# Decoder kernel: gates and scan of the next group moved between the down products, in buffers of their own

## The reference, cut

```
xn = rmsnorm(x);  left = gelu(xn @ left_W)
r = conv4(xn @ right_W)                 # causal, depthwise
a = exp(-8 softplus(a_param) * sigmoid(r @ ga_W));  i = sigmoid(r @ gx_W)
h_t = a_t h_(t-1) + sqrt(1 - a_t^2) * (i_t * r_t)   # scan along the sequence
x1 = left * h @ out_W + x
y  = (gelu(x1n @ up1_W) * (x1n @ up2_W)) @ down_W + x1 ;  x2 = layernorm(y)

kv = products of ctx features in heads of 8;  conv over 128 positions with a
per-head kernel;  out = sum with the query x2 ;  x3 = layernorm(x2 + out)

scores = softmax(x3 @ gate_w.T); top 6 of 64 experts, 64 tokens an expert;
shared expert (352 wide, silu) + 64 experts (176 wide); layernorm
```

## Time and profile before

| | us |
|---|---|
| median of 3 runs | 564.67 (563.73 to 568.37) |
| the profiled execution | 562.52, its span 560.7 |
| TensorE busy | 516.0 (92%) |
| VectorE busy | 377.3 (67%) |
| ScalarE busy | 216.9 (39%) |
| POOL busy | 193.1 (34%) |
| mean granted clock | 0.986 |

### The profile page before, as it was taken

The page is one execution under the profiler, slowest core; times in us unless marked ns, Lnnn a source line. Parts: engine busy times, 40 slices in busy tenths (PEclk is TensorE's granted clock), DMA queues, the critical chain, the costliest instruction groups (busy, mean ns, idle before and its releaser), DMA issues.

```text
span 560.7 us, 6906 instructions
## 1 busy us (share of the span) xinstructions
PE 516.0 (92%) x2211; PEld 317.7 (57%) x2211; DVE 377.3 (67%) x953; ACT 216.9 (39%) x440; POOL 193.1 (34%) x236
## 2 busy tenths in 40 slices
PE   7999999999999799999979999987879999998876
PEld 3438466754766554587744668754444555554565
DVE  2653246759775959786877975899855666663296
ACT  5484135722346841225844114610303333332043
POOL 4703400139024237021507303100026677744250
PEclk9999999999999989999989999998998999999999
DMA  7900993000001100010700010599997999996997
GB/s 269 338 3 23 414 402 136 1 25 13 2 0 39 56 15 23 1 39 0 249 1 1 0 37 2 193 316 294 272 264 231 322 337 331 317 314 221 374 417 260
DMA packets 39894, 91.83 MB, mean 164 GB/s; under 512 B 4513, under 2 KB 24385, under 8 KB 39729
## 3 DMA queue, kind: packets, MB, share of 16 engines
q1 hardware_dynamic: 34864, 75.45, 40.4%
q0 software_dynamic: 4992, 15.93, 8.8%
HBM read 67.02 MB, written 24.34 MB: 163 GB/s over the span
## 4 chain that ended last, share of the span: by engine, by line
PE 65%; DVE 22%; DMA 5%; issue 5%; ACT 2%; SPq 1%; POOL 0%; DVEq 0%; POOLq 0%
PE mb L781 17%; PE mb L1080 8%; PE kb L974 8%; DMA arena<-y_dram 4%; PE kb L1100 4%; PE kb L920 3%; PE kb L1098 3%; PE kb L809 2%; DVE arena L1160 2%; PE mb L787 2%; PE tb L787 2%; DVE arena L1146 2%; PE kb L800 2%; PE mb L800 2%; PE mb L832 2%
## 5 line engine op out<-in xcount | busy, mean ns | idle before, releaser
L781 PE MATMUL mb<-arena 128*128 128x512 f32 x320 | 140.2, 594 | 6.1 <-DVE arena L1201 5.4
L781 PEld LDWEIGHTS mb<-arena 128*128 128x128 f32 x320 | 60.3, 190 | 78.2 <-issue 69.6
L443 POOL TENSOR_TENSOR arena<-arena 128x256 f32<-128x256 f32 (+7 forms) x128 | 80.9, 665 | 66.2 <-PE mb L834 66.2
L673 ACT ACTIVATE arena<-mb,cols 128x512 f32<-128x512 f32 x24 | 16.5, 687 | 78.0 <-PE mb L781 77.9
L974 PE MATMUL kb<-arena 128*128 128x256 f32 x192 | 44.2, 381 | 1.9 <-DVE arena L1389 1.7
L974 PEld LDWEIGHTS kb<-arena 128*128 128x128 f32 x192 | 35.5, 190 | 9.5 <-DVE arena L1389 4.6
L1080 PE MATMUL mb<-arena,x3T 128*64 128x352 f32 x224 | 39.3, 472 | 0.0
L507 POOL DMA_INDIRECT y_dram<-shh,y_all x32 | 32.2, 1008 | 19.9 <-DVE shh L1539 12.2
L468 POOL TENSOR_TENSOR arena<-arena 128x1024 f32<-128x1024 f32 x4 | 9.4, 2350 | 84.6 <-DVE arena L1196 58.9
L1160 DVE TENSOR_TENSOR arena<-arena 128x1024 f32<-128x1024 f32 x28 | 35.9, 1284 | 0.5
L1389 DVE SCALAR_TENSOR_TENSOR arena<-mb,cols,arena 128x512 f32<-128x512 f32 x24 | 17.9, 744 | 24.0 <-PE mb L781 24.0
(11 more groups left out here) (243 smaller groups left out, 1016.3 us busy)
## 6 DMA issues: line engine op xcount, KB each, us to landing
arena<-in_w_experts_dram SPq DMA_DIRECT2D x28, 704.0 KB, 14.8
y_dram<-zeros SPq DMA_DIRECT2D x16, 768.0 KB, 11.0
arena<-y_dram SPq DMA_DIRECT2D x16, 768.0 KB, 16.7
arena<-in_w_experts_down_dram SPq DMA_DIRECT2D x56, 128.0 KB, 13.9
rows_dram<-rows POOLq DMA_DIRECT2D x4, 768.0 KB, 7.0
wextra<-in_w_experts_dram SPq DMA_DIRECT2D x4, 704.0 KB, 6.5
arena<-in_w_experts_down_dram SPq DMA_DIRECT2D x28, 96.0 KB, 14.6
arena<-in_x_dram SPq DMA_DIRECT2D x4, 512.0 KB, 3.6
```

The source lines that it names most:

```text
L443: last = e.tensor_tensor(v.kv[:, hb % 2, :, :, DOFF[d] * NB:DOFF[d] * NB + n], cx[:, :, :, 0:n], cx[:, :, :, d * NB:d * NB + n], ALU.mult)
L781: last = e.matmul(bank, w[:, c, n0:n0 + P], rhs[:, c, :], start=(c == 0), stop=(c == C - 1))
```

## The change

The gates, recurrence and scan of the next group run at the end of a step, in buffers of their own (in `wextra`, where the first two expert weights are loaded later, so these loads now wait for the last scan). A step opens with shared_up 0 (or three fillers), x2's transposes and the out products; heads 8 to 15 follow them. Shared_up 1 and 2 follow x1's transposes. The eight rounds of a group are spread: four in the up stretch of VectorE, four behind `residual(0)`. `products(gt, 3)` runs in the next step's beginning, `biased` before `products(gh, 2)`, and load_ctx follows load_x in SP's queue. PSUM banks are dealt out anew to fit. Group 0's gates and scan stay in step 0.

```diff
-        v.ri = v.mlp[:, 0:4, :]
-        v.th = v.mlp[:, 4:6, :]
+        at[0] = 0
+        v.ri = take(2 * C * TG, wextra).rearrange("p (c n) -> p c n", c=2 * C)
+        v.th = take(C * TG, wextra).rearrange("p (c n) -> p c n", c=C)
+        v.hs = take(C * TG, wextra).rearrange("p (c n) -> p c n", c=C)
@@ sync_program
-                wait(e, s["xs_s"], 2 * g)
+                wait(e, s["xs_s"], 2 * g - 1)
...
-        load_ctx(1)
         for g in range(2, G):
             load_x(g)
-            load_ctx(g)
+            load_ctx(g - 1)
+        load_ctx(G - 1)
...
+        e.wait_ge(s["lr_s"], C * G)
         for p in range(2):
             load_pair(p, v.ring[p], f"load{p}")
@@ pool_program, step
+            if gt is not None:
+                if gh is not None:
+                    wait(e, s["x2_s"], 4 * gh)
+                products(gt, 3)
...
+                if gh + 1 < G:
+                    wait(e, s["xs_s"], 2 * gh + 2)
+                    biased(gh + 1)
...
                 products(gh, 2)
-                products(gh, 3)
-                if gh + 1 < G:
-                    biased(gh + 1)
@@ act_program, step: order of a full step now
   sdA, chances(gs) [Exp of the logits], silu_shared 0, table, mean_square(x1), rms2,
   conv_out(gt, 8..15), norm_root(gh+1), silu_shared 1 and 2, 6 Gelu, conv_out(gh, 0..1),
   sdB, left_right(gh+1), conv_out(gh, 2..3), recurrence(gh+1) [sigmoids, Tanh, Exp],
   x3T copies, roots(gh+1), conv_out(gh, 4..7)
@@ pe_program, step
             if head and tail:
+                wait(e, s["gate_s"], 4 * gh + 4)
+                wait(e, s["conv_evac"], HEADS * gt + 8)
+                if gs is not None:
+                    shared_up(gs, 0, [(s["gate_s"], 4 * gh + 4)] * 2, head)
+                else:
+                    keep_clock(mb[2], 3)
                 x2_transposes()
...
                 wait(e, s["lr_s"], C * gh + C)
                 e.wait_ge(s["w_out"], 16)
-                if tail:
-                    wait(e, s["conv_evac"], HEADS * gt + 14)
+                wait(e, s["y_s"], 2 * gh)
...
+                    for h in range(8, 16):
+                        if h >= 12:
+                            wait(e, s["conv_evac"], HEADS * gt + h - 3)
+                        elif h >= 10 and gs is not None:
+                            wait(e, s["shg_s"] if h == 10 else s["shh_s"], NF * gs + 1)
+                        conv(gt, h)
...
+            if head and gh + 1 < G:
+                features(gh + 1)
             (transposes of the query result, heads 0 and 1)
                 if gh + 1 < G:
+                    if tail:
+                        wait(e, s["conv_evac"], HEADS * gh + 2)
+                    left_right(gh + 1)
                 down([(0, 1)], True)
...
+                    conv(gh, 2)
+                    conv(gh, 3)
+                if gh + 1 < G:
+                    gates(gh + 1)
                 down([(1, 0)], False)
             (x3's transposes, logits, heads 4 to 7, each behind gate_s)
                 down([(1, 1)], True)
@@ dve_program, step
             if head:
+                x1_sum(0)
                 if gs is not None:
+                    shared_rows(gs, 0, head)
+                x1_sum(1)
+                (the query's two copies)
...
+                    if j == 4 and gh + 1 < G:
+                        norm_one(gh + 1)
...
+                    if gs is not None and j < 4:
+                        rounds(j, j + 1)
...
             if head:
                 residual(0)
             if gs is not None:
+                rounds(4, 8)
                 keep_first()
+            if head and gh + 1 < G:
+                recurrence(gh + 1)
             (the logits' maximum)
+            if head and gh + 1 < G:
+                scan(gh + 1, 0)
             if head:
                 n = hsteps.did(residual(1))
             (statistics, lnA_s)
+            if head and gh + 1 < G:
+                scan(gh + 1, 1)
```

More of the change, by code:

```diff
@@ L653, in step @@
                     silu_shared(gs, 1, head)
+                    silu_shared(gs, 2, head)
             if head:
@@ L696, in step @@
                         .then_inc(s["x3T_s"], 1)
+            if head and gh + 1 < G:
+                roots(gh + 1)
             if head and tail:
-                conv_out(gh, 6)
-                conv_out(gh, 7)
-            if tail:
-                wait(e, s["logit_read"], gt + 1)
-                e.activation(v.logit[:], v.logit[:], ACT.Exp).then_inc(s["exp_s"], 1)
+                for h in range(4, 8):
+                    conv_out(gh, h)
+            if tail and not head:
+                chances(gt)
         over_groups(e, step)
@@ L888, in step @@
                 votes_by_expert(gs)
-            if gs is not None and head:
-                shared_up(gs, 0, [(s["q_s"], 2 * gt + 2)] * 2, head)
-                wait(e, s["conv_evac"], HEADS * gt + 15)
-                wait(e, s["dve_r"], RDVE * gt)
-                votes_by_expert(gs, head)
-            elif gs is not None:
+            if gs is not None and not head:
                 for f in range(2):
@@ L940, in step @@
                     transposes(v.xn, k, "x1_tr")
+                if gs is not None:
+                    shared_up(gs, 1, [(s["x1_s"], 2 * gh + 2)] * 2, head)
                 if not tail:
@@ L946, in step @@
                 e.wait_ge(s["w_up"], 16)
+                if gs is not None:
+                    shared_up(gs, 2, [(s["x1T_s"], 4 * gh + 4)] * 2, head)
                 for j in range(FJ):
@@ new lines, in scan @@
+            def scan(g, c):
+                a, i = v.ri[:, 0:2, :], v.ri[:, 2:4, :]
+                wait(e, s["mult_s"], C * g + c + 1)
+                n = csteps.did(e.tensor_tensor(v.th[:, c, :], v.th[:, c, :], i[:, c, :], ALU.mult))
+                wait(e, csteps.sem, n)
+                n = csteps.did(e.tensor_tensor_scan(v.hs[:, c, :], a[:, c, :], v.th[:, c, :], 0.0, ALU.mult, ALU.add))
+                wait(e, csteps.sem, n)
+                wait(e, s["left_s"], 2 * g + c + 1)
+                e.tensor_tensor(v.left[:, c, :], v.left[:, c, :], v.hs[:, c, :], ALU.mult).then_inc(s["lr_s"], 1)
@@ L1315, in step, with x1_sum @@
+            def x1_sum(k):
+                wait(e, s["out_done"], 2 * gh + k + 1)
+                wait(e, s["xo_s"], gh + 1)
+                e.tensor_tensor(v.xo[:, 2 * k:2 * k + 2, :], kb[k][:].rearrange("p (b n) -> p b n", b=2),
+                                v.xo[:, 2 * k:2 * k + 2, :], ALU.add).then_inc(s["x1_s"], 1)
             if head and not tail:
                 row_convolution(0)
+                recurrence(0)
+                for c in range(C):
+                    scan(0, c)
+                csteps.end()
@@ L1365, in step @@
                 norm_apply(v.xn, v.xo, v.inv2, "x1n_s")
+                if gs is not None:
+                    votes_in(gs, head)
                 for k in range(2):
@@ L1402, in step @@
                     f()
-            if head and gh + 1 < G:
-                norm_one(gh + 1)
-            if gs is not None:
-                rounds(3 if head else 2, 5 if head else 4)
+            if gs is not None and not head:
+                rounds(2, 4)
             if head and gh + 1 < G:
```

272 lines of the change are left out of this document (116 added, 156 removed).

## The result

| | before | after |
|---|---|---|
| median of 9 runs each, same chip, us | 564.67 (563.73 to 568.37) | 571.57 (569.37 to 575.19) |
| ratio after/before | | 1.0106, interval 1.0078 to 1.0133 |
| the profiled execution (span) | 562.52 (560.7) | 572.56 (570.5) |
| mean granted clock | 0.986 | 0.974 |

The change costs 1.1%. Ratios leave out the few executions that were over 1.5% above the fastest of their kernel. The profiled executions differ by 10.0 us, the medians by 6.9. One early event and one late one give a measure that ends before the first gather: from VectorE's copy of the turned features at the end of step 0 (78.83) to the transposes of the picks at the end of the loop. I call it **the loop**. It takes 335.6 us before (78.83 to 414.41) and 341.9 after (78.67 to 420.57): 6.3 us more.

What follows compares the result with a forecast made beforehand. Most of a step was taken as TensorE work, with a scan hole of 5.5 us in steps 2 and 3. Terms 1.3 + 2.0 + 1.3 + 0.9 + 0.9 - 1.4 - 1.4 + 0.2 = +3.8 us gave 568, range 560.5 to 576.

Steps and rivals of the forecast that it cites:

- The hole: TensorE's idle in the openings, expected before x2's transposes instead of out: 3.1 us in steps 2 and 3, 7.8 in step 1.
- The closings: First down product to next gates: left/right wait for head copies and x3; +0.9 us each in steps 1 and 2.
- the end of step 0: Left/right products no longer have a down half ahead while VectorE copies the turned features; TensorE idles, +1.3 us.
- Openings of steps 2 and 3: Gates to first up product: only the second half scan delays x2; 27.2 us instead of 28.6, -1.4 each.
- Opening of step 1: x2 waits for the whole scan, TensorE idles 7.8 us; length unchanged, plus 2.0 us for the lower clock afterwards.
- Up stretches of steps 2 and 3 ... 0: Four rounds and norm_one add 5.8 us on VectorE, covered by an earlier start and TensorE's chain: 0, cover thin.
- the +1.3 in step 1: Up stretch of step 1, bound by VectorE: norm_one before the fifth hidden product counts whole, +1.3 us.
- rival 2: VectorE becomes the bound of the up stretches: 573 us, 576 with contention in openings; chance 0.26 together with Rival 4.
- Signs: Expected in the trace: D near 186 to 188, VectorE over 95% in three up stretches; wrong if step 2's exceeds 29 us.
- Rival 1: The clock holds in the openings of steps 2 and 3: +1.0 instead of +3.8 us, 565.7 us; chance 0.20.
- Rival 3: The second half scan runs ahead of D, so x2 comes at D + 4: -7 us, 557.5 us; chance 0.10.
- Rival 4: Out still waits for the scan, behind x2, no gain in steps 2 and 3: 571 us; 0.26 together with rival 2.

Runs made afterwards that it cites:

- e2: The changed kernel with both halves of the scan ahead of the last residual on VectorE; ratio 1.0016 to the kernel before, loop 336.5 us.
- e1: The changed kernel with POOL's biased moved back behind products(gh, 2); ratio 1.0042 to the kernel before, loop 336.4 us.
- e3: The changed kernel with 11 fillers instead of 3 in step 1 and three more behind shared_up 0 in steps 2 and 3; ratio 1.0024 to the kernel before.
- e5: The changed kernel with norm_one moved back behind VectorE's hidden products; ratio 1.0053 to the kernel before, loop 338.8 us.
- e8: The kernel before, unchanged, profiled once more in the second session; loop 335.1 us against 335.6 in its first trace.
- e6: The changed kernel with biased and norm_one back, both scan halves ahead of the residual, and 11 fillers for 3 in step 1; ratio 0.9934 to the kernel before.
- e11: The same program as e6, run again in the third session; ratio 0.9921 to the kernel before, median 575.72 us, loop 332.5 us.
- e9: The changed kernel, word for word, run again in the third session; ratio 1.0108 to the kernel before, loop 342.0 us.

## Why the prediction was right or wrong

The forecast was 568 within [560.5, 576], so 3.3 us slower than before. Measured are 571.6, in the range and slower, but by 6.9 us, twice the forecast, and just outside the forecast's own spread of 564 to 571. The chances had put 0.62 on within 1% and 0.28 on slower than that; 1.06% [0.78, 1.33] lies on the line between them. In the loop the sum was +3.8 and the measurement +6.3. The terms that came out dearer make +4.0, and 1.5 came back in others, most of it in the openings of steps 2 and 3.

**Right, by mechanism.** The hole moves from out to x2, with 3.1 and 7.8 us forecast and 2.62 and 7.58 measured. The closings were right by 0.1, the end of step 0 by 0.2. e2 shows the cause the prediction gave: take the second half scan from between statistics and x2, and the openings lose 2.2 us each.

**Openings of steps 2 and 3: -2.0 instead of -1.4.** Without slow clock and without a price for POOL the prediction had 25.5; e1's step 3 and e3 measured 25.53. The slow clock adds 1.07 net and not 1.4. The other 0.3 is what the 25.8 held for POOL beside top_six, and that was not there. (The prediction says 0.6 in one place, but 25.8 is only 0.3 above 25.5.) POOL's products did run beside it, 4.18 us instead of 3.43 for x8, but the votes' transposes at 208.65 waited for nothing.

**Mis-sized: "Opening of step 1", with +2.0 for the clock.** It was +3.3. The price came from the earlier trace rows, where only out stood behind the idle. In the new order x2's transposes stand there too: 1.97 instead of 1.04 and 5.54 instead of 3.62 make 2.85, and the rest is smaller waits. e3 gave 2.8 back with fillers alone.

**Failed: "Up stretches of steps 2 and 3 ... 0", and the +1.3 in step 1.** norm_one was right (e5: 1.28). What the sum left at 0 was `biased`. The prediction held its POOL price at 0 to 1.6 "in an up stretch" and put it into rival 2 only. Measured: 2.05 us in step 1, 1.2 in step 2, none in step 3, where no group follows and there is no `biased`. So half of rival 2 came true inside the forecast's case. The row of L1329 was the right kind of evidence but not its ceiling: the wide L1154 lost 2.04 (3.53 against 1.49), more than L1329's 1.6. The rule of the Trainium skill cited there (GPSIMD Engine Reference, section 1, shared memory interfaces and instructions with two inputs) fits: in e2's step 2 the loss went when POOL's instruction stood beside the rounds, in e1 when it stood elsewhere, and in the changed kernel L1269 (0.60 instead of 0.43, two inputs) suffered beside POOL while nothing waited for it.

**Signs.** D, the end of the last down half, came at 190.0 and not at 186 to 188, by the two misses in step 1. VectorE was busy 99% of the up stretches of steps 1 and 2 but 92% of step 3's, not over 95% in all three. The up stretch of step 2 took 28.89 us, just under the 29 that would have told the prediction wrong.

**Rival 1** (the clock holds) depends on the execution: the same idle of 2.6 us left 1.09 and 3.62 in e1's step 3, and 1.74 and 4.68 here. **Rival 3** did not occur, for the reason the prediction gave (the order on VectorE); e2 made that order. **Rival 4** is refuted by the rows above. The profiled execution was read against 562.5, but 3.5 of its +10.0 belong to the gather, which no step named. In the medians +6.9 is the loop's 6.3 and 0.6 that I can't assign.

## What to carry to other kernels

When a stalled chain is moved ahead of other work on the same in-order engine, ask which half of it stands before the next thing that is waited for; here half a scan (2.6 us) in the wrong place cost 2.2 us twice, half of it through the clock, and ahead of the residual it cost 0.4 us once. A hole costs its length and then the slower products behind it, and fillers give back the second part at once, so try them before reordering. When a change removes fillers, put their worth into the sum: 8 fillers back in step 1 were worth 2.8 us. An instruction on a helper engine that is "off the path" is priced by what it runs beside: put it next to narrow or one-input work, and give it a number in the sum, not only in a rival.

## What the hardware showed unexpectedly

**The clock after equal idles.** Products behind idles of 7.6 and 8.1 us were always slow (seven traces). Behind 2.6 us they were slow in eight of ten cases and fast in two (e1, step 3; e5, step 2). Even the kernel before, after 3.53 us in step 3, took 3.72 for out in e8 and 5.41 in its first trace. Behind 1.2 us out took 3.62 in all nine cases.

**A drop with hardly any idle.** In e3 and e6 TensorE ran slower for some 3.5 us in the closing of step 2 (convolution products 0.48 us apart instead of 0.25), where it had waited only 0.93 us for the copies of x3. TensorE in e6:

```profile
269.13 0.61 PE L844 MATMUL mb<-arena 128*128 128x144 f32 x2
269.53 0.69 PE L845 MATMUL mb<-arena 128*128 128x144 f32 x2
...
273.00 0.41 PE L844 MATMUL mb<-arena 128*128 128x144 f32 x2
```

The closing took 38.20 us at a granted clock of 0.96. e11, the same program, took 36.54 at 1.00 behind the same wait. e11 lost 1.1 us in step 4 instead (64.4 against e6's 63.3 from the end of step 3's last down half to the picks). There the slow products came behind 1.53 us of idle; in e6 they had come earlier, on fillers (3.46 us for x4 instead of 1.88), where little waits for them. TensorE row of e11, and the changed kernel's for the same products:

```profile
393.30 5.40 PE L811 MATMUL mb<-x3T,wsh 128*128 128x512 f32 x8 [1.53 <-DVE logit L1475]
```
```profile
402.42 3.70 PE L811 MATMUL mb<-x3T,wsh 128*128 128x512 f32 x8 [0.98 <-DVE logit L1476]
```

So up to 1.7 us of one stage of one trace can be chance, and stages should be compared in more than one trace. The Trainium skill (TensorE: Matmul & The Clock Gate, What's actually happening) says that the monitor's period is not tied to the program's start, so the same kernel can change rate at another place in another run; these traces agree.

**Contention depends on a microsecond of offset.** POOL's 128x1024 instruction took 3.33 us beside L1154 and 2.35 elsewhere, and L1154 3.79 instead of 1.83 in step 2. In the changed kernel and e9 POOL starts 1.15 us ahead of that product. In e2 and e5 it starts 2.2 and 2.6 us behind it, and both numbers are the undisturbed ones without any edit to POOL; only the end of its 2.35 us met a narrower L1154 (128x512), which took 1.10 and 1.45 instead of 0.68.

The rows look like taking turns, not like sharing. In step 1 of the changed kernel POOL begins at 140.98 beside L1168, which ends at 142.1; 2.35 us later is 144.4, and POOL ends at 144.3. L1154, begun at 142.13, ends at 145.66, 1.35 us after POOL, and alone it takes 1.49. In e2's step 2 L1154 came first and kept its 1.83 us, and the two small POOL products beside it took 2.04 us:

```profile
221.07 2.04 POOL L443 TENSOR_TENSOR arena<-arena 128x64 f32<-128x64 f32 x2
```

The same two took 0.52 in e1. What moved POOL by 3.3 us against VectorE's order is in part the 16 products ahead of `biased`: 10.8 us in the changed kernel and e9, 13.3 in e2 and 13.4 in e5. Why they took longer there stays open.
